# Linear attention with key sums from a constant channel, key-value products through the weights, and no token-major v

## The chip, the cores and the metric

The kernel is written for one Trainium2 chip and runs on one of its cores. The metric is the device time of one execution in microseconds. An execution has one launch and ends when the last output block has been written to HBM. The profile is of one such execution; its engines are TensorE (PE, with its weight loads apart as PEld), VectorE (DVE), ScalarE (ACT), GpSimd (POOL) and SyncE (SP), which here only issues transfers.

## The reference

The input is 32 sequences of 256 tokens with 128 channels, all float32. One transformer layer is computed:

```
h   = layernorm(x)                       # over the 128 channels, no gain, no offset
q,k,v = h Wq^T, h Wk^T, h Wv^T           # 8 heads of 16
q,k = rope(q), rope(k)
kv  = sum_s k_s v_s^T ; ksum = sum_s k_s ; vsum = sum_s v_s     # per sequence and head
a_s = (q_s kv / 4 + vsum) / (q_s . ksum / 4 + 256)
o   = (a + depthwise_conv5(v) + lepe_b) * (h Wg^T)
x2  = x + o Wo^T
out = x2 + (fp8 product of layernorm(x2) with the 128x128 ffn weights, to bf16) + ffn_b
```

Two identities are at work in the change. Layernorm output sums to zero over its channels, so W h does not change if the same column is subtracted from every column of W; with column 0 subtracted, channel 0 no longer counts and may hold anything. And with vm = vsum / 256, a_s = vm + (q_s (kv - ksum vm^T) / 4) / (q_s . ksum / 4 + 256).

## The kernel before, in words

A unit u is two sequences, that is four tiles of 128 tokens; there are 16 units (U). Every stage is a small helper of one engine that takes u, waits on semaphores for its inputs and for its buffers to come free, works on all of the unit and signals. The order in which an engine calls its helpers is written out by hand in each of the five engine blocks (`@block.tensor`, L1079 on, and so on): a beginning with its own order, a loop in the middle (`for t in range(6, 12)` on TensorE, L1320, with `project_g(t - 3)` as its first call), and the last units written out again. So TensorE works at the same time on units t, t - 1, t - 2, t - 3 and t - 4, and each queue runs strictly in its order.

The stages of one unit, with the engine and the line of the helper's work:

- SyncE loads x (`load_x`, L240) into one of four slots and stores the result (`store`).
- `stats1` (VectorE, L803) takes mean and variance, `var_eps1` (ScalarE, L293/L294) prepares them, `pow1` (GpSimd, L543/L546) computes 1/sqrt and the offset, `norm1` (ScalarE, L303) writes h, token-major.
- `transpose_h` (TensorE, L1112) turns it; `move_hT` (ScalarE, L315) copies it to SBUF channel-major as hT, two halves of 256 tokens, and sums each over the tokens as it goes (hsum).
- `project_qk` (TensorE, L1122), once for each sequence j: hT tiles as weights, 256 columns of joint q and k weights moving, token-major result. `rope` (VectorE, L812) multiplies by cosines and sines, `add_rope` (GpSimd, L583) adds the pairs.
- `project_v` (TensorE, L1133): four products with hT tiles as weights, giving v token-major; `move_v` (ScalarE, L323) copies it to SBUF; `transpose_v` (TensorE, L1149) turns it into v channel-major in PSUM, on which the five-tap convolution works: `conv_outer` and `conv_middle` (ScalarE, L333, L342), three `conv_tap` (VectorE, L827) and `sum_outer` (GpSimd, L595). `conv_middle` adds lepe_b as its bias.
- `transpose_q` (L1157) and `move_qT` (ScalarE, L349) give q channel-major.
- `key_value` (TensorE, L1168): k tiles as weights against v with eight columns of ones beside it, accumulated over two tiles of a sequence, so kv and ksum in one; `mask_kv` (VectorE, L838) keeps the blocks of each head.
- `sum_v` (TensorE, L1179) writes vsum to all tokens of the numerator: hsum broadcast as weights, twice 272 columns moving, `start=True`; `attend` (L1187) adds q kv on it with `start=False`. `invert` (VectorE, L844/L847) takes 1/den, `divide` (L854) gives t1.
- `transpose_t1` (TensorE, L1196), `add_lepe` (VectorE, L862), `project_g` (TensorE, L1141, one 512-column product), `gate` (VectorE, L871), `project_o` (TensorE, L1206), `residual` (VectorE, L879).
- The second half: `stats2` (L889), `var_eps2`, `pow2` (L554), `norm2` (L367), `transpose_h2` (L1215), `quantise_if_small` (L398), `ffn` (L1249), `move_y` (L405), `add_bias` (L602), `final_sum` (L609).

A product of float32 tiles shows as two matmul instructions with a weight load each, a transpose as one. PSUM has eight banks. The numerator p_num has two of its own; the other six are shared by turns between the rest, and the extra waits that TensorE's calls carry, as in

```
project_v(t - 1, (hT_done, count_first(t - 1)))
transpose_v(t - 1, (tap_done[-1], count(t - 2)))
sum_v(t - 2, (t1_done, count_last(t - 3)))
attend(t - 2)
```

name who must have read a bank before it is written again. VectorE's loop is `stats1(t)`, `add_lepe(t-3)`, `gate(t-3)`, `rope(t-1,1)`, `mask_kv(t-2)`, `residual(t-3)`, `stats2(t-3)`, `conv_tap(t-1,0)`, `rope(t-1,0)`, `invert(t-2)`, `conv_tap(t-1,1)`, `divide(t-2)`, `conv_tap(t-1,2)`. ScalarE's is `norm2`, `move_v`, `quantise_if_small`, `var_eps1`, `conv_middle`, `move_y`, `conv_outer`, `norm1`, `move_qT`, `var_eps2`, `move_hT`. At the start SyncE issues its transfers in the order x of unit 0 in two halves, ident, turn (the cosines and sines, 512 KB), wo, x of unit 1, conv_w, conv_b, mask, four small loads for the ffn, x of unit 2, x of unit 3; ScalarE's queue issues wq, wk, wv, wg. TensorE first keeps itself busy with 13 products of zeros, then turns the weights (L1088 to L1095).

## Time and profile before

| | |
|---|---|
| time, median of 3 runs | 175.99 us (175.90 to 176.16) |
| time of the profiled execution | 175.88 us |
| its span, first to last instruction | 174.1 us |
| TensorE busy | 161.3 us (93%), 1140 instructions |
| VectorE busy | 151.9 us (87%), 281 |
| GpSimd busy | 137.1 us (79%), 163 |
| ScalarE busy | 132.5 us (76%), 358 |
| chain that ended last | TensorE 83%, VectorE 6% |
| mean granted clock of TensorE | 0.976 |

Times are microseconds from the start of the span. A matmul's duration in the trace includes the time until its result is in PSUM, so neighbours overlap; what one costs in a full stream is the difference between starts. The same holds, by about 0.1 us, for ScalarE. "Idle before <- releaser" is the wait ahead of a group of instructions and who ended it.

### The profile page before, as it was taken

What the parts mean: (1) busy time and instruction counts of PE and PEld (TensorE: products, weight loads), DVE (VectorE), ACT (ScalarE), POOL (GpSimd) and SP (SyncE); (2) the same over time, 40 slices, a digit from 0 to 9 for tenths busy, and PEclk for the clock granted to TensorE, in tenths of its full rate; (3) what the DMA queues carried; (4) which work ended last, traced back from release to release, by engine and by line L of the source; (5) the groups of instructions that cost most, each with busy time, mean ns of one, the idle gap of its engine ahead of it and who ended that gap; (6) DMA issues with size and microseconds to landing.
All of it is one profiled execution on the core that took longest, in us unless ns stands there. A gap on an engine that the chain in (4) does not pass through costs nothing.

```text
span 174.1 us, 3891 instructions
## 1 busy us (share of the span) xinstructions
PE 161.3 (93%) x1140; PEld 137.5 (79%) x1140; DVE 151.9 (87%) x281; ACT 132.5 (76%) x358; POOL 137.1 (79%) x163
## 2 busy tenths in 40 slices
PE   7796999999999999999999999999999999998740
PEld 2475799797989898998989898989987897977510
DVE  2279999989998999999999999899898999999734
ACT  3668495787988878896969888676867797796671
POOL 1438698888989888989898888996979568987871
PEclk9999999999999999999999999999999999999955
DMA  4840002004040404021030404030040210100224
GB/s 121 241 122 0 0 6 60 2 0 124 2 120 6 120 0 120 6 76 48 21 101 0 124 2 120 6 101 20 2 124 0 85 43 0 49 15 2 60 60 121
DMA packets 18966, 9.71 MB, mean 56 GB/s; under 512 B 1536, under 2 KB 18816, under 8 KB 18944
## 3 DMA queue, kind: packets, MB, share of 16 engines
q1 hardware_dynamic: 18368, 9.19, 18.3%
q10 hardware_dynamic: 576, 0.26, 0.6%
q8 instruction: 10, 0.16, 0.4%
q14 instruction: 12, 0.10, 0.2%
HBM read 5.25 MB, written 4.19 MB: 54 GB/s over the span
## 4 chain that ended last, share of the span: by engine, by line
PE 83%; DVE 6%; SPq 3%; issue 2%; DMA 2%; POOL 1%; ACT 1%; DVEq 0%; ACTq 0%; POOLq 0%
PE bank L1122 14%; PE p_num L1187 9%; PE bank L1168 8%; PE bank L1206 8%; PE p_num L1179 8%; PE bank L1133 8%; PE bank L1141 8%; PE bank L1157 4%; PE bank L1196 4%; PE bank L1149 4%; PE bank L1112 4%; DMA xs<-_attn_hidden_states_dram 2%; PE bank L1249 2%; PE bank L1215 2%; DVE turned L812 1%
## 5 line engine op out<-in xcount | busy, mean ns | idle before, releaser
L583 POOL TENSOR_TENSOR qk<-turned 128x512 f32<-128x512 f32 x32 | 40.3, 1275 | 2.4 <-DVE turned L812 2.2
L812 DVE TENSOR_TENSOR turned<-bank,turn 128x1024 f32<-128x1024 f32 x32 | 38.6, 1215 | 0.7 <-PE bank L1122 0.3
L827 DVE SCALAR_TENSOR_TENSOR acc<-bank,conv_w,acc 128x510 f32<-128x510 f32 (+1 forms) x48 | 34.7, 722 | 0.5 <-ACT acc L342 0.4
L1122 PE MATMUL bank<-w_qk,hT 128*128 128x256 f32 x128 | 32.7, 380 | 0.0
L367 ACT ACTIVATE h<-x,nmr,rs 128x128 bf16<-128x128 f32 x60 | 24.7, 482 | 6.4 <-POOL nmr L557 6.3
L303 ACT ACTIVATE h<-xs,nmr,rs 128x128 f32<-128x128 f32 x64 | 26.3, 486 | 0.7 <-POOL nmr L546 0.7
L543 POOL TENSOR_TENSOR rs<-ve,minus_half 128x4 f32<-128x4 f32 (+1 forms) x17 | 16.6, 975 | 10.7 <-ACT ve L294 10.5
L595 POOL TENSOR_TENSOR acc<-acc,outer 128x508 f32<-128x508 f32 x16 | 20.3, 1268 | 5.8 <-DVE acc L827 5.7
L1122 PEld LDWEIGHTS bank<-w_qk,hT 128*128 128x128 f32 x128 | 22.4, 191 | 2.4 <-issue 0.2
L554 POOL TENSOR_TENSOR rs<-ve,minus_half 128x4 f32<-128x4 f32 (+1 forms) x17 | 16.6, 977 | 8.5 <-ACT ve L358 8.5
L1133 PEld LDWEIGHTS bank<-w_v,hT 128*128 128x128 f32 x128 | 16.5, 192 | 5.0 <-issue 4.3
L1187 PE MATMUL p_num<-kvs,qT 128*128 128x136 f32 x128 | 18.2, 284 | 0.4 <-DVE kvs L838 0.4
L602 POOL TENSOR_TENSOR yc<-yb,fb 128x512 bf16<-128x512 bf16 x15 | 17.3, 1153 | 1.2 <-ACT yb L405 1.2
L609 POOL TENSOR_TENSOR ob<-x,yc 128x512 f32<-128x512 f32 x15 | 17.4, 1159 | 0.9
L1206 PE MATMUL bank<-w_o,oT 128*128 128x128 f32 x128 | 17.3, 277 | 0.8 <-DVE oT L871 0.8
L1168 PE MATMUL bank<-v,qk 128*128 128x136 f32 x128 | 17.7, 281 | 0.1
L1179 PE MATMUL p_num<-w_v,hsum 128*128 128x272 f32 x64 | 17.4, 394 | 0.0
L398 ACT ACTIVATE q<-bank,rsc 128x512 fp8e4<-128x512 bf16 x15 | 10.3, 685 | 9.3 <-PE bank L1215 9.3
L1133 PE MATMUL bank<-w_v,hT 128*128 128x128 f32 x128 | 16.9, 275 | 0.0
L1187 PEld LDWEIGHTS p_num<-kvs,qT 128*128 128x128 f32 x128 | 16.1, 190 | 0.9 <-issue 0.8
L1206 PEld LDWEIGHTS bank<-w_o,oT 128*128 128x128 f32 x128 | 15.7, 192 | 1.3 <-DVE oT L871 1.3
L1141 PE MATMUL bank<-hT,w_g 128*128 128x512 f32 (+1 forms) x34 | 16.4, 570 | 0.0
(88 smaller groups left out, 326.6 us busy)
## 6 DMA issues: line engine op xcount, KB each, us to landing
xs<-_attn_hidden_states_dram SPq DMA_DIRECT2D x15, 256.0 KB, 2.8
out_dram<-ob SPq DMA_DIRECT2D x15, 256.0 KB, 2.5
turn<-in_turn_dram SPq DMA_DIRECT2D x1, 512.0 KB, 5.3
xs<-_attn_hidden_states_dram SPq DMA_DIRECT2D x2, 128.0 KB, 2.7
out_dram<-ob SPq DMA_DIRECT2D x2, 128.0 KB, 2.1
mask<-in_mask_dram SPq DMA_DIRECT2D x1, 68.0 KB, 4.3
w_raw<-in_L_attn_Wq_dram ACTq DMA_DIRECT2D x1, 64.0 KB, 2.3
w_raw<-in_L_attn_Wk_dram ACTq DMA_DIRECT2D x1, 64.0 KB, 2.4
```

The costliest lines, as they stand in the source:

```text
L303: last = nc.scalar.activation(h[:, s, t], xs[:, u % NX, t], ACT.Identity, scale=rs1[:, s, t:t + 1], bias=nmr1[:, s, t:t + 1])
L367: last = nc.scalar.activation(h2[:, s, t], x2[:, u % 3, t], ACT.Identity, scale=rs2[:, s, t:t + 1], bias=nmr2[:, s, t:t + 1])
L583: nc.gpsimd.tensor_tensor(qk[:, u % 2, j].rearrange("p q t d -> p t q d"), turned[:, j, :, :, 0:D].rearrange("p a h (q d) -> p (a h) q d", ...
L812: nc.vector.tensor_tensor(turned[:, j], p_qk[j].rearrange("p a h d -> p a (h d)").unsqueeze(2).to_broadcast([P, TPB, 2, 2 * D]), turn[:], ...
L827: nc.vector.scalar_tensor_tensor(out=part, in0=p_vT[:, :, lo + off:hi + off], scalar=conv_w[:, k:k + 1], in1=part, op0=ALU.mult, op1=ALU.a ...
L1122: last = nc.tensor.matmul(p_qk[j][:, a].rearrange("p h d -> p (h d)"), hT[:, u % 3, t * P:(t + 1) * P], w_qk[:].rearrange("p a q d -> p (a ...
L1133: last = nc.tensor.matmul(p_v[:, t], hT[:, u % 3, t * P:(t + 1) * P], w_v[:, 0:D], start=True, stop=True)
L1141: nc.tensor.matmul(p_gT[:] if j is None else p_end_gT[j], w_g[:], hT[:, u % 3, part_of(j)], start=True, stop=True).then_inc(gT_filled, 1)
L1168: last = nc.tensor.matmul(p_kv[:, t // TPB], qk_tile(u, 1, t), v[:, u % 3, t], start=(t % TPB == 0), stop=(t % TPB == TPB - 1))
L1179: nc.tensor.matmul(p_num[:, TPB * j:TPB * (j + 1), 0:NW], hsum[:, u % 3, j:j + 1].to_broadcast([P, P]), w_v[:].unsqueeze(1).to_broadcast([ ...
L1187: last = nc.tensor.matmul(p_num[:, t, 0:NW], qT[:, u % 2, t * P:(t + 1) * P], kvs[:, u % 2, t // TPB], start=False, stop=(t % TPB == TPB - 1))
L1206: last = nc.tensor.matmul(dst[:, n], oT[:, u % 2, t * P:(t + 1) * P], w_o[:], start=True, stop=True)
```

## The change

- `norm1` writes channels 1 to 127 of h only; channel 0 of all slots is set to one at the start, and h has three slots. The weights Wq, Wk, Wv and Wg have their column 0 subtracted on VectorE before they are turned (`subtract_first`, four instructions).
- `project_v` is one product with w_v as weights and 512 columns of hT moving, whose result is v channel-major in PSUM. `move_v`, `transpose_v` and the tile v are gone.
- `sum_v` computes the sum of v twice: as rows (33 output partitions, 128 columns) and as columns (128 partitions, 2 columns). `move_row` (ScalarE) writes the rows, times -1/256, into row 0 of w_kv, a copy of w_v per slot and sequence with eight more columns that are 1 in row 0 and 0 elsewhere. `move_col` writes lepe_b plus the columns over 256 into `bias`, which `conv_middle` adds, now as one instruction per sequence.
- `gather` (TensorE) takes h token-major as weights against k: kh, 128 channels by 128, per sequence, in which row 0 is the sum of k; `move_kh` (ScalarE) copies it; `key_value` is one product kh x w_kv per sequence, which gives kv - ksum vm^T and the sum of k in the eight columns.
- `attend` has no base written before it (`start=True`).
- PSUM is one tensor of eight banks with new sharing: kh is in bank 0 and q turned in bank 1, the two banks of p_num; `project_qk(.,0)` has bank 4, `project_qk(.,1)` bank 2 with t1 turned and the ffn result; the sums bank 5; kv, hT and h2 turned bank 7; the gate and `project_o` bank 6; v bank 3.
- All engines have new orders, SyncE's first loads too.

The diff, cut to its core:

```diff
@@ SyncE, first loads
             sp.dma_start(ident[:], ident_c).then_inc(wqk_in, 16)
+            for dst, src in ((conv_w[:], lepe_w.rearrange("c a k -> c (a k)")),
+                             (conv_b[:], lepe_b.rearrange("(c a) -> c a", a=1))):
+                sp.dma_start(dst, src).then_inc(c_in, 16)
             sp.dma_start(turn[:], turn_c).then_inc(turn_in, 16)
-            sp.dma_start(w_raw[:, 4], wo).then_inc(w_in, 16)
             load_x(1)
...
+            load_x(2)
+            sp.dma_start(mask[:], mask_c).then_inc(c_in, 16)
+            sp.dma_start(w_raw[:, 4], wo).then_inc(wo_in, 16)
@@ ScalarE
-                    last = nc.scalar.activation(h[:, s, t], xs[:, u % NX, t], ACT.Identity, scale=rs1[:, s, t:t + 1],
-                                                bias=nmr1[:, s, t:t + 1])
+                    last = nc.scalar.activation(h[:, u % 3, t, 1:D], xs[:, u % NX, t, 1:D], ACT.Identity,
+                                                scale=rs1[:, s, t:t + 1], bias=nmr1[:, s, t:t + 1])
...
-            def move_v(u):
...
+            def move_row(u):
+                act.wait_ge(vsum_filled, count(u))
...
+                for b in range(BPU):
+                    last = nc.scalar.activation(w_kv[0:1, u % 2, b, 0:D], p_vsum[ROW * b:ROW * b + 1, 0:D], ACT.Copy,
+                                                scale=-1.0 / S)
+                last.then_inc(row_done, 1)
+
+            def move_col(u):
...
+                nc.scalar.activation(bias[:, u % 2], p_vsum[:, D:D + BPU], ACT.Identity, scale=1.0 / S,
+                                     bias=conv_b[:, 0:1]).then_inc(col_done, 1)
+
+            def move_kh(u):
+                act.wait_ge(kh_filled, count(u))
+                if u >= 2:
+                    act.wait_ge(kv_filled, count(u, 2))
+                nc.scalar.activation(kh[:, u % 2], p_kh, ACT.Copy).then_inc(kh_done, 1)
...
-                nc.scalar.activation(acc[:, u % 2], p_vT, ACT.Identity, scale=conv_w[:, TAPS // 2:TAPS // 2 + 1],
-                                     bias=conv_b[:, 0:1]).then_inc(tap2_done, 1)
+                act.wait_ge(col_done, count(u))
+                for b in range(BPU):
+                    last = nc.scalar.activation(acc[:, u % 2, b], p_vT[:, b], ACT.Identity,
+                                                scale=conv_w[:, TAPS // 2:TAPS // 2 + 1],
+                                                bias=bias[:, u % 2, b:b + 1])
+                last.then_inc(tap2_done, 1)
@@ ScalarE, loop
-            for t in range(5, 12):
+            for t in range(6, 12):
                 norm2(t - 4)
-                move_v(t - 1)
+                move_col(t - 1)
                 quantise_if_small(t - 4, is_small)
                 var_eps1(t)
+                conv_outer(t - 1)
                 conv_middle(t - 1)
                 move_y(t - 4)
-                conv_outer(t - 1)
+                move_kh(t - 2)
+                move_qT(t - 2)
                 norm1(t)
-                move_qT(t - 2)
                 var_eps2(t - 3)
+                move_row(t - 1)
                 move_hT(t)
@@ GpSimd
+            def set_up_w_kv():
+                pool.wait_ge(v_ready, 1)
+                nc.gpsimd.tensor_copy(w_kv[:, :, :, 0:D].rearrange("p a b d -> p (a b) d"),
+                                      w_v[:].unsqueeze(1).to_broadcast([P, 2 * BPU, D])).then_inc(w_kv_done, 1)
...
+            for t in range(5, 12):
+                pow1(t)
+                add_bias(t - 4)
+                final_sum(t - 4)
+                pow2(t - 3)
+                add_rope(t - 1, 1)
+                add_rope(t - 1, 0)
+                sum_outer(t - 1)
@@ VectorE
+            def subtract_first(n):
+                nc.vector.tensor_scalar(w_diff[:, n], w_raw[:, n], w_raw[:, n, 0:1], None,
+                                        ALU.subtract).then_inc((diff_qk_done, diff_vg_done)[n // 2], 1)
...
             stats1(0, 0)
             stats1(0, 1)
+            difference_qk()
+            difference_vg()
             set_up_qk()
             set_up_v()
             set_up_g()
             stats1(1)
+            rope(0, 0)
+            stats1(2)
+            rope(0, 1)
             set_up_o()
-            stats1(2)
-            rope(0, 0)
-            rope(0, 1)
...
+            for t in range(6, 13):
                 stats1(t)
                 add_lepe(t - 3)
                 gate(t - 3)
-                rope(t - 1, 1)
-                mask_kv(t - 2)
+                rope(t - 1, 0)
+                conv_tap(t - 1, 0)
                 quantise_if_wide(t - 4, is_small)
                 residual(t - 3)
+                mask_kv(t - 2)
                 stats2(t - 3)
-                conv_tap(t - 1, 0)
-                rope(t - 1, 0)
+                rope(t - 1, 1)
                 invert(t - 2)
                 conv_tap(t - 1, 1)
                 divide(t - 2)
                 conv_tap(t - 1, 2)
@@ TensorE
-                for t in range(TPU):
-                    last = nc.tensor.matmul(p_v[:, t], hT[:, u % 3, t * P:(t + 1) * P], w_v[:, 0:D], start=True, stop=True)
-                last.then_inc(v_filled, 1)
+                nc.tensor.matmul(p_vT.rearrange("p j s -> p (j s)"), w_v[:], hT[:, u % 3], start=True,
+                                 stop=True).then_inc(vT_filled, 1)
...
+                nc.tensor.matmul(p_vsum[0:ROW + 1, 0:D], hsum[:, u % 3], w_v[:], start=True, stop=True)
+                nc.tensor.matmul(p_vsum[:, D:D + BPU], w_v[:], hsum[:, u % 3, ::ROW], start=True,
+                                 stop=True).then_inc(vsum_filled, 1)
...
+            def gather(u, *freed):
...
+                for t in range(TPU):
+                    last = nc.tensor.matmul(p_kh[:, t // TPB], h[:, u % 3, t], qk_tile(u, 1, t),
+                                            start=(t % TPB == 0), stop=(t % TPB == TPB - 1))
+                last.then_inc(kh_filled, 1)
...
+                for b in range(BPU):
+                    last = nc.tensor.matmul(p_kv[:, b], kh[:, u % 2, b], w_kv[:, u % 2, b], start=True, stop=True)
+                last.then_inc(kv_filled, 1)
@@ TensorE, loop
             for t in range(6, 12):
                 project_g(t - 3, (x2_done, count_last(t - 4)))
-                project_v(t - 1, (hT_done, count_first(t - 1)))
-                project_qk(t - 1, 1, (rope_done[1], count(t - 2)))
-                transpose_t1(t - 3, (qT_done, count(t - 3)))
-                transpose_h2(t - 4, (v_done, count(t - 1)))
-                transpose_v(t - 1, (tap_done[-1], count(t - 2)))
-                key_value(t - 2, (rope_done[0], count(t - 2)))
-                ffn(t - 4, is_small, (q8_done, count(t - 4)))
-                transpose_q(t - 2, (t2_done, count_last(t - 3)))
+                project_qk(t - 1, 0, (rope_done[0], count(t - 2)))
+                sum_v(t - 1, (row_done, count(t - 2)), (col_done, count(t - 2)))
+                transpose_t1(t - 3, (rope_done[1], count(t - 2)))
+                transpose_h2(t - 4, (hT_done, count_first(t - 1)))
+                project_v(t - 1, (tap_done[-1], count(t - 2)))
+                transpose_q(t - 2, (t1_done, count_last(t - 3)))
+                ffn(t - 4, is_small, (t2_done, count_last(t - 3)))
+                gather(t - 2, (t1_done, count_last(t - 3)))
                 project_o(t - 3, (oT_done, count_last(t - 3)))
-                sum_v(t - 2, (t1_done, count_last(t - 3)))
-                project_qk(t - 1, 0, (kvs_done, count(t - 2)))
-                transpose_h(t, (yb_done, count(t - 4)))
-                attend(t - 2)
+                key_value(t - 2, (q8_done, count(t - 4)))
+                project_qk(t - 1, 1, (yb_done, count(t - 4)))
+                attend(t - 2, (kh_done, count(t - 2)), (qT_done, count(t - 2)))
+                transpose_h(t, (kvs_done, count(t - 2)))
@@ TensorE, last unit
-            project_g(15, (tap_done[-1], count(15)), j=0)
-            project_g(15, (rope_done[1], count(15)), j=1)
-            transpose_t1(15, (qT_done, count(15)), j=0)
+            project_g(15, (rope_done[0], count(15)), j=0)
+            key_value(15, (q8_done, count(12)))
             project_o(14, (oT_done, count_last(14)))
-            attend(15, 0)
-            transpose_h2(13, (yb_done, count(12)))
-            attend(15, 1)
-            ffn(13, is_small, (q8_done, count(13)))
+            attend(15, (kh_done, count(15)), j=0)
+            transpose_h2(13, (kvs_done, count(15)))
+            attend(15, (qT_done, count(15)), j=1)
+            transpose_t1(15, (t1_done, count_last(15, j=0)), j=0)
+            ffn(13, is_small, (t2_done, count_last(14)))
             transpose_t1(15, (x2_done, count_last(14)), j=1)
+            project_g(15, (q8_done, count(13)), j=1)
+            project_o(15, (yb_done, count(13)), j=0)
```

## Rows read from the trace of the kernel before

**Rows 1.** By stretch: us; TensorE, its loads, VectorE, ScalarE, GpSimd busy; clock, DMA share, GB/s.

```profile
0.00:11.65 11.65, 9.50 (x41) 5.71 (x42) 3.65 (x12) 5.75 (x17) 3.50 (x16) 1.00 0.67 181
11.65:31.00 19.35, 17.41 (x118) 14.65 (x118) 18.56 (x34) 14.35 (x42) 14.71 (x20) 1.00 0.05 15
31.00:106.70 75.70, 75.48 (x560) 67.16 (x559) 72.13 (x128) 64.59 (x176) 66.57 (x71) 1.00 0.19 55
106.70:161.04 54.34, 53.51 (x392) 46.70 (x392) 50.72 (x95) 41.35 (x108) 44.73 (x48) 1.00 0.13 39
161.04:174.10 13.06, 5.35 (x32) 3.29 (x32) 6.83 (x17) 6.42 (x16) 7.58 (x11) 0.68 0.28 80
```

**Rows 2.** TensorE in order of time, one unit: start, duration, line, tile, count.

```profile
87.67 1.02 PE L1141 MATMUL bank<-hT,w_g 128*128 128x512 f32 x2
88.53 1.05 PE L1133 MATMUL bank<-w_v,hT 128*128 128x128 f32 x8
89.42 1.03 PE L1122 MATMUL bank<-w_qk,hT 128*128 128x256 f32 x4
90.29 0.60 PE L1196 MATMUL bank<-ident,t 128*128 128x128 f32 x4
...
90.95 0.61 PE L1149 MATMUL bank<-ident,v 128*128 128x128 f32 x4
91.39 1.09 PE L1168 MATMUL bank<-v,qk 128*128 128x136 f32 x8
92.32 0.39 PE L1249 MATMUL bank<-fwq,q 128*128 128x128 bf16 x4
...
93.02 1.06 PE L1206 MATMUL bank<-w_o,oT 128*128 128x128 f32 x8
93.92 1.08 PE L1179 MATMUL p_num<-w_v,hsum 128*128 128x272 f32 x4
94.83 1.03 PE L1122 MATMUL bank<-w_qk,hT 128*128 128x256 f32 x4
95.70 0.60 PE L1112 MATMUL bank<-ident,h 128*128 128x128 f32 x4
96.13 1.13 PE L1187 MATMUL p_num<-kvs,qT 128*128 128x136 f32 x8
97.10 1.02 PE L1141 MATMUL bank<-hT,w_g 128*128 128x512 f32 x2
```

**Rows 3.** ScalarE in order of time, the same unit.

```profile
89.83 0.57 ACT L323 ACTIVATE v<-bank 128x512 f32<-128x512 f32 x1
...
92.08 0.77 ACT L342 ACTIVATE acc<-bank,conv_b,conv_w 128x512 f32<-128x512 f32 x1
...
93.33 0.68 ACT L333 ACTIVATE outer<-bank,conv_w 128x508 f32<-128x508 f32 x1
...
96.33 0.38 ACT L315 ACTIVATE hT<-bank 128x256 f32<-128x256 f32 x1
...
96.97 0.20 ACT L315 ACTIVATION_READ_ACCUMULATOR hT<-bank 128x1 f32 x1
```

**Rows 4.** VectorE in order of time, the same unit; in brackets the idle time before.

```profile
93.39 0.43 DVE L838 TENSOR_TENSOR kvs<-bank,mask 128x272 f32<-128x272 f32 x1
94.12 0.69 DVE L879 TENSOR_TENSOR x<-bank,xs 128x512 f32<-128x512 f32 x1 [0.29 <-PE bank L1206]
```

**Rows 5.** VectorE in order of time, the start; in brackets the wait and its releaser.

```profile
10.97 0.76 DVE L803 BATCH_NORM_STATS2 st<-xs 128x6 f32<-128x256 f32 x2 [1.26 <-DMA xs<-_attn_hidden_states_dram]
11.65 2.34 DVE L812 TENSOR_TENSOR turned<-bank,turn 128x1024 f32<-128x1024 f32 x2
```

**Rows 6.** SyncE's queue in order of time: the issues of x of units 2 and 3.

```profile
7.07 0.98 SPq L240 DMA_DIRECT2D xs<-_attn_hidden_states_dram  x2
```

**Rows 7.** DMA issues: queue, count, KB, us from issue to landing.

```profile
w_raw<-in_L_attn_Wg_dram ACTq DMA_DIRECT2D x1, 64.0 KB, 4.8
```

**Rows 8.** VectorE in order of time, the end.

```profile
162.40 0.42 DVE L862 TENSOR_TENSOR t<-bank,acc 128x256 f32<-128x256 f32 x1 [0.79 <-PE bank L1196]
```

715 lines of the change are left out of this document (366 added, 349 removed).

## The prediction

> **What bounds the kernel now.** I read the stretches first, then TensorE's order of time, then the other engines beside it. From 31 to 106.7 us TensorE is busy 75.48 of 75.70 us, VectorE 72.13, GpSimd 66.57 and ScalarE 64.59 [rows 1]. That stretch is eight units (a unit is two sequences, 512 tokens), so TensorE is the bound, and VectorE is only 0.4 us a unit behind it. One unit of the repeated schedule takes 97.10 - 87.67 = 9.43 us between two starts of the gate projection [rows 2], with no hole in it. On VectorE the same unit shows one wait, 0.29 us for `project_o` [rows 4]; so VectorE alone would need 9.43 - 0.29 = 9.14 us for a unit, and that is the first floor under whatever TensorE saves. Two other places matter: the start, where VectorE's first `rope` begins at 11.65 us, and the end, 13.06 us in which TensorE is mostly idle [rows 1].
>
> **TensorE's work, part by part.** Times are differences of starts in [rows 2], since the engine is pipelined. `project_v` goes from 8 instructions of 128 columns (89.42 - 88.53 = 0.89) to one 512-column product, for which `project_g` is the row: 88.53 - 87.67 = 0.86. `transpose_v` goes: 91.39 - 90.95 = 0.44. `key_value` falls from four tiles to two products of the same shape, 0.93 to 0.47, but `gather` is new: four accumulating 128-column tiles, as the old `project_v`, 0.90. `sum_v` falls from four passes of 272 columns (94.83 - 93.92 = 0.91) to one 128-column pair (0.22) and one pair of two columns. No row has two columns; it costs nothing if it hides wholly, and at most what a 128-column pair costs, 0.22, plus 0.10 if the load behind it shows. I take 0.24, near the top, because the weights it loads are full tiles. Sum before 0.89 + 0.44 + 0.93 + 0.91 = 3.17, after 0.86 + 0.47 + 0.90 + 0.46 = 2.69: 0.48 us less a unit, 8.95 in place of 9.43, and 7.7 us over sixteen units. All other products keep their shapes.
>
> In the trace weight loads cost almost nothing beside a product: `project_g` streams its 512 columns with 2 loads in 0.86, the old `project_v` the same columns with 8 loads in 0.89 [rows 2]. The Trainium skill, TensorE: Matmul & The Clock Gate, section Measured speedup vs the span model, says a load overlaps a running matmul only where the two use different row groups. By that rule the six loads a unit that go (24 to 18) would give back their own time too, about 0.1 us each, and the unit would fall by some 0.6 us more; these rows, all of full tiles, speak against it, and the sum would be the same by both, since TensorE is no longer the bound after the change.
>
> **ScalarE.** `move_v` (0.57 [rows 3], some 0.50 of it its own after overlap) goes. `move_kh` copies half as much: the half-width copy of `move_hT` takes 0.38, some 0.28 of it its own. `move_row` is two instructions of 128 elements on one partition, `move_col` one of two elements; the bounds are the one-element 0.20 and the 256-element 0.38 [rows 3], and with the overlap of neighbours I take 0.2 each, 0.6 together, near the short row. `conv_middle` in two halves: 0.77 as one, so two of about 0.55 that overlap by 0.1, 0.25 more. Net 0.28 + 0.60 + 0.25 - 0.50 = 0.63 more a unit. ScalarE was busy 64.59 / 8 = 8.07 us a unit [rows 1], so 8.7: still under the others, but no longer loose.
>
> The Trainium skill, ScalarE: Activation LUTs, section What ACT_TABLE_LOAD costs, states 186 ns plus 0.833 ns per element, 93 ns more for each per-partition pointer, and 93 ns of overlap. By it one `move_row` instruction would occupy 200 ns, and a half of `conv_middle` 490 ns, which puts the split at 0.31 us more rather than 0.25; the row of the whole (0.77) stands a little under the page's figure for it (0.80). By the page the sum would be 0.06 x 12 = 0.7 us longer, if ScalarE lies on the ring.
>
> **VectorE and GpSimd.** Their work a unit is unchanged; GpSimd's is 66.57 / 8 = 8.3 us. Once, at the start, VectorE subtracts column 0 from four weight matrices, each 128 columns, so under the 0.43 of `mask_kv` with 272 [rows 4] and over nothing; I take 0.25, 1 us together, most of it in time in which it waits for data (3.65 busy of 11.65 [rows 1]). GpSimd's copy of w_v into four slots (512 columns) I put at 1.2 us, over the 66.57 / 71 = 0.94 of its mean instruction, which takes the tiny ones in [rows 1]; it lies in an idle stretch (3.50 busy of 11.65) but is queued ahead of `pow1(1)`, so unit 1's normalisation waits for it, and its transposes for that.
>
> **Does the saving reach the end?** TensorE's 8.95 is under VectorE's 9.14, so VectorE or a ring of waits sets the unit. I follow two rings through the new loop. The first starts when `mask_kv` has ended: `attend` 0.97, `transpose_h` 0.43, `move_hT` (96.13 to 97.17 [rows 2, 3]) 1.04, `project_qk` half 0 0.87, `sum_v` 0.46, `transpose_t1` and `transpose_h2` 90.95 - 90.29 = 0.66, `project_v` 0.86, `ffn` and `transpose_q` 93.02 - 92.32 = 0.70, `gather` 0.90, `project_o` 0.90, 0.20 until `residual` starts, then 0.69 for it and 0.43 for `mask_kv` [rows 4]: 9.1 us. In it TensorE waits 0.2 us for `move_hT`, because only `project_g` (0.86) stands between the transposes and their use, where before `attend` stood there too. The second leaves through ScalarE: after `project_v` 0.2, `conv_outer` 0.68 less 0.10 of overlap, then `conv_middle` and `move_y` 93.33 - 92.08 = 1.25 with 0.25 more for the split, `move_kh` 0.38 and 0.05 to be seen, `key_value` 0.47, `project_qk` half 1 0.87, then `attend` to `project_v` as above, 0.97 + 0.43 + 1.04 + 0.87 + 0.46 + 0.66 + 0.86: 9.3 us. So three things stand between 9.1 and 9.3; I take 9.25, 0.18 below now.
>
> **The sum.** Eight units at 0.18: 1.4. From 106.70 to 161.04, four to five units in a hand-written order, VectorE idles 54.34 - 50.72 = 3.6 us while TensorE has 53.51 of work [rows 1]; TensorE's share falls by 4 x 0.48 = 1.9, and I take two thirds, 1.3. From 11.65 to 31, VectorE idles 0.8: 0.2 of it. Start: `rope(0,0)` stands behind `stats1(2)`, which waits until 10.97 for a load issued only at 7.07 [rows 5, 6]. The change issues it six slots earlier and puts the first `rope` ahead of it. On SP's queue `turn` is then two slots later, about 1 us (0.98 for two issues [rows 6]), `load_x(1)` one and `wo` five, with its transpose taken out of the first chain; `mask` keeps its slot. What then ends last is the gate matrix, whose differences VectorE takes before it copies w_qk out: it is the fourth issue of ScalarE's queue, so issued near 2.1, and lands 4.8 later [rows 7], near 7; then `set_up_qk` near 7.8, first product 7.9, `rope` about 9.1, against 11.65. VectorE must also do `stats1(2)` (0.7) later, so the stream is 1.8 us ahead; bounds are 0 (the wait for the new gate-weight chain eats it) and 2.5 (all of it). End: `transpose_t1` is no longer behind both gate products, for which VectorE waited 0.79 [rows 8]: 0.5. Together 1.4 + 1.3 + 0.2 + 1.8 + 0.5 = 5.2 us. The profiled execution took 175.88 (span 174.10 and 1.78 around it), 0.11 under the median of 175.99; the sum from it is 170.7, from the median 170.8.
>
> **Rivals.** (a) VectorE's holes close fully. The units run at 9.14 (8 x 0.29 = 2.3), the late stretch gives 2.5, the start 2.3, the end 0.8: with 0.3 early, 8.2 us, about 167.8. For it: the orders of all engines are new. Against: both rings above are as long as VectorE's work, and each hand-over has to be met. (b) Only the start and the end gain. The unit stays at 9.43, since a ring takes TensorE's place exactly: 2.3 to 2.8 us, about 173.5. For it speaks how near 9.3 is to 9.43. (c) Slower: the ScalarE ring. One bank now holds first `kh`, then attention's numerator, and TensorE's in-order queue has `key_value` ahead of `project_qk`, `attend` and the next transposes, so each 0.1 us by which `move_kh` is late is 0.1 us a unit. Its reasons to be late are three small instructions and a split ahead of it. At a third of a microsecond more than my 9.3 the ring is 9.63; over twelve units that is 2.4 us lost, with no gain in the late stretch, against 1.0 gained at the start if that is short too: 177.4. It decides where twelve units' excess over 9.43 passes what start and end gain: from 9.51 a unit with 1.0 gained, from 9.62 with the 2.3 of my sum. Against it: these are instructions of 0.2 us, and ScalarE has over 0.5 us a unit idle. (d) The change doesn't do what it says for TensorE: the two-column product or a bank handed back late costs what was saved, TensorE stays the bound at 9.4, and the start is eaten by the longer weight chain: about 175.9.
>
> **How the numbers follow.** Forecast 0.60, at 170.8, its own range 169.2 to 172.6; (a) 0.15; (b) 0.12; (c) 0.10; (d) 0.03. The range takes in (b) and most of (a) and the low end of (c): 168.0 to 175.2. About 0.2% (0.35 us) is what a measurement of this kernel can tell from no change: faster 0.85 (forecast, (a), (b) less a little), same 0.04, slower 0.11.
>
> **What would show it.** Right: two starts of `project_g` in the middle of the loop 9.2 to 9.3 us apart; TensorE busy about 7 to 8 us less in all, with a hole of 0.2 us ahead of the first `project_qk` of a unit; VectorE busy over 97% there, its 0.29 us wait gone or under 0.1; `transpose_v` and `move_v` absent, `gather` at 0.90, `sum_v` near 0.46; the first `rope` near 9.1 us. Wrong: a period of 9.4 or more, with waits of TensorE on `kh` or of ScalarE on the sums; a first `rope` after 10.5; or a second product of `sum_v` that holds TensorE for 0.4 us.

## The result and the profile after

The changed kernel takes 178.38 us (median of 4 runs, 178.29 to 178.56) beside 175.94 for the kernel before (4 runs on the same chip): ratio 1.0137, interval 1.0121 to 1.0153. It is slower by 2.4 us, where 170.8 was forecast and 168.0 to 175.2 was the range. The profiled execution took 178.29, of which the span is 176.4.

From the page of the kernel after, its first line of busy times and its chain:

```profile
PE 162.9 (92%) x1044; PEld 122.2 (69%) x1044; DVE 152.4 (86%) x285; ACT 143.4 (81%) x422; POOL 138.5 (78%) x166
PE 72%; ACT 9%; issue 6%; DVE 6%; POOL 5%; ACTq 1%; DVEq 0%; POOLq 0%
```

TensorE has 96 instructions fewer and is busy 1.6 us longer than before (161.3). Its share of the last chain fell from 83% to 72%: 9% now leads through ScalarE and 6% is "issue". The middle stretch of [rows 1] on the kernel after (window and length; then busy time and count of PE, PEld, DVE, ACT, POOL; granted clock, DMA share, GB/s):

```profile
31.00:106.70 75.70, 73.91 (x490) 56.60 (x489) 69.35 (x122) 67.45 (x197) 63.44 (x68) 1.00 0.17 50
```

In the middle TensorE now idles 1.8 us, and yet VectorE does less in that stretch than before (69.35 against 72.13): fewer units pass. The granted clock is 1.00 there before and after, so it has no part in this.

The steady loop shows why. One unit of TensorE in order of time (start, duration, engine, line, operation, tile, shape, count):

```profile
88.40 0.60 PE L1189 MATMUL psum<-ident,h 128*128 128x128 f32 x4
88.84 1.02 PE L1226 MATMUL psum<-hT,w_g 128*128 128x512 f32 x2
89.93 1.13 PE L1199 MATMUL psum<-w_qk,hT 128*128 128x256 f32 x4
90.99 0.41 PE L1217 MATMUL psum<-w_v,hsum 128*33 128x128 f32 x2
91.33 0.38 PE L1218 MATMUL psum<-hsum,w_v 128*128 128x2 f32 x2
91.57 0.64 PE L1272 MATMUL psum<-ident,t 128*128 128x128 f32 x4
92.05 0.39 PE L1291 MATMUL psum<-identb,h 128*128 128x128 bf16 x4
92.27 1.08 PE L1209 MATMUL psum<-hT,w_v 128*128 128x512 f32 x2
93.19 0.60 PE L1234 MATMUL psum<-ident,qk 128*128 128x128 f32 x4
93.62 0.39 PE L1325 MATMUL psum<-fwq,q 128*128 128x128 bf16 x4
94.08 1.13 PE L1243 MATMUL psum<-qk,h 128*128 128x128 f32 x8
95.04 1.06 PE L1282 MATMUL psum<-w_o,oT 128*128 128x128 f32 x8
95.94 0.69 PE L1255 MATMUL psum<-w_kv,kh 128*128 128x136 f32 x4
96.46 1.03 PE L1199 MATMUL psum<-w_qk,hT 128*128 128x256 f32 x4
```

The next `project_g` starts at 98.71: 9.87 us a unit, against 9.43 before [rows 2] and 9.25 forecast. (These are single units from the middle of the loop; over the seven units from `divide(3)` to `divide(10)` the means are 9.83 and 9.51, so the loop as a whole lost 0.32 a unit.) By differences of starts: `project_g` 1.09, first `project_qk` 1.06, the two products of `sum_v` 0.58, `project_v` 0.92, `transpose_q` and ffn 0.89, `gather` 0.96, `key_value` 0.52. From [rows 2] I had priced them at 0.86, 0.87, 0.46, 0.86, 0.70, 0.90 and 0.47. The loads of the same unit say what stood there:

```profile
89.93 0.73 PEld L1199 LDWEIGHTS psum<-w_qk,hT 128*128 128x128 f32 x4 [0.90 <-ACT hT L335]
90.99 0.14 PEld L1217 LDWEIGHTS psum<-w_v,hsum 128*33 128x33 f32 x2 [0.33 <-issue]
94.05 0.97 PEld L1243 LDWEIGHTS psum<-qk,h 128*128 128x128 f32 x8 [0.21 <-issue]
```

The load for `project_qk` comes only when `move_hT` has signalled, 0.90 after the last load and when `project_g` (88.84 + 1.02) is over, so it lies beside no product; in the kernel before, `attend` stood in between and covered it. ScalarE in the same unit (start, duration, engine, line, tile):

```profile
89.04 0.38 ACT L335 ACTIVATE hT<-psum 128x256 f32<-128x256 f32 x1 [0.21 <-PE psum L1189]
...
89.41 0.38 ACT L335 ACTIVATE hT<-psum 128x256 f32<-128x256 f32 x1
...
93.40 0.67 ACT L371 ACTIVATE outer<-psum,conv_w 128x508 f32<-128x508 f32 x1
93.97 1.02 ACT L382 ACTIVATE acc<-psum,bias,conv_w 128x256 f32<-128x256 f32 x2
...
95.44 0.40 ACT L361 ACTIVATE kh<-psum 128x256 f32<-128x256 f32 x1
```

`move_kh` ends at 95.84 and `key_value` starts at 95.94, 0.90 after `project_o`, which is what `project_o` costs anyway: TensorE's own queue and the way through ScalarE arrive together. VectorE waits three times, where [rows 4] had one wait of 0.29:

```profile
92.25 0.69 DVE L960 TENSOR_TENSOR t<-psum,acc 128x512 f32<-128x512 f32 x1 [0.18 <-PE psum L1272]
95.02 0.75 DVE L925 SCALAR_TENSOR_TENSOR acc<-psum,conv_w,acc 128x510 f32<-128x510 f32 x1 [0.23 <-ACT acc L382]
96.14 0.69 DVE L977 TENSOR_TENSOR x<-psum,xs 128x512 f32<-128x512 f32 x1 [0.36 <-PE psum L1282]
```

The three waits are 0.77, and 9.87 less 0.77 is 9.10, so VectorE's list still is the 9.14 of the forecast. One hand-over from it is tight all the same: `residual` waits for `project_o` and starts at 96.14, `mask_kv` behind it ends at 97.17, and `attend`, which needs its result, loads its weights at 97.24.

Where the 2.3 us of span came from, by the starts of `divide` in both traces (there is one `divide` for each unit, numbered from 0, and the last is in two halves):

| stretch | before | after | difference |
|---|---|---|---|
| start to `divide(2)` | 42.17 | 40.08 | -2.1 |
| `divide(2)` to `divide(3)` | 8.99 | 10.61 | +1.6 |
| `divide(3)` to `divide(10)` | 66.58 | 68.82 | +2.2 |
| `divide(10)` to the last one | 43.45 | 44.70 | +1.3 |
| last `divide` to the end | 12.9 | 12.2 | -0.7 |

In unit 3 TensorE's order of time has two holes, around the hand-over from the beginning to the loop:

```profile
40.16 1.13 PE L1199 MATMUL psum<-w_qk,hT 128*128 128x256 f32 x4 [0.47 <-ACT hT L335]
47.29 1.09 PE L1263 MATMUL psum<-kvs,qT 128*128 128x136 f32 x8
48.69 0.65 PE L1189 MATMUL psum<-ident,h 128*128 128x128 f32 x4 [0.31 <-ACT h L322]
```

By the starts, `project_g` takes 1.49 there (38.67 to 40.16) where 0.86 is its row, and `transpose_h` starts 1.40 after `attend`, which takes 0.92 in the loop: about 1.1 us in the two.

### The profile page after: what moved, and what is told of

It is laid out like the page before. It is cut to its first block, busy times and chain, and to the rows that moved or that the text cites. A ratio compares the mean times of both kernels' runs of the same rounds, so it can differ in the third digit from the quotient of the medians.

```text
span 176.4 us, 3817 instructions
## 1 busy us (share of the span) xinstructions
PE 162.9 (92%) x1044; PEld 122.2 (69%) x1044; DVE 152.4 (86%) x285; ACT 143.4 (81%) x422; POOL 138.5 (78%) x166
## 4 chain that ended last, share of the span: by engine, by line
PE 72%; ACT 9%; issue 6%; DVE 6%; POOL 5%; ACTq 1%; DVEq 0%; POOLq 0%
PE psum L1199 15%; PE psum L1243 8%; PE psum L1209 8%; PE psum L1263 7%; PE psum L1282 7%; PE psum L1255 4%; PE psum L1189 4%; PE psum L1272 4%; PE psum L1234 3%; PE psum L1217 3%; ACT hT L335 3%; PE psum L1218 3%; PE psum L1226 3%; ACT h L322 2%; PE psum L1325 2%
## 5 line engine op out<-in xcount | busy, mean ns | idle before, releaser
L910 DVE TENSOR_TENSOR turned<-psum,turn 128x1024 f32<-128x1024 f32 x32 | 38.8, 1213 | 1.2 <-PE psum L1199 1.2
L925 DVE SCALAR_TENSOR_TENSOR acc<-psum,conv_w,acc 128x510 f32<-128x510 f32 (+1 forms) x48 | 34.7, 722 | 2.7 <-ACT acc L382 2.0
L1199 PE MATMUL psum<-w_qk,hT 128*128 128x256 f32 x128 | 34.2, 390 | 1.1 <-ACT hT L335 0.7
L1199 PEld LDWEIGHTS psum<-w_qk,hT 128*128 128x128 f32 x128 | 21.9, 190 | 10.4 <-ACT hT L335 8.3
L322 ACT ACTIVATE h<-xs,nmr,rs 128x127 f32<-128x127 f32 x64 | 26.5, 500 | 0.8 <-POOL nmr L624 0.8
L1243 PE MATMUL psum<-qk,h 128*128 128x128 f32 x128 | 17.6, 281 | 1.0 <-issue 0.7
L1263 PE MATMUL psum<-kvs,qT 128*128 128x136 f32 x128 | 18.0, 282 | 0.0
L1282 PE MATMUL psum<-w_o,oT 128*128 128x128 f32 x128 | 17.4, 277 | 0.1
L1209 PE MATMUL psum<-hT,w_v 128*128 128x512 f32 x32 | 16.9, 611 | 0.0
L1226 PE MATMUL psum<-hT,w_g 128*128 128x512 f32 (+1 forms) x34 | 16.7, 572 | 0.1
```

Of the source, the lines that this page charges most:

```text
L322: last = nc.scalar.activation(h[:, u % 3, t, 1:D], xs[:, u % NX, t, 1:D], ACT.Identity, scale=rs1[:, s, t:t + 1], bias=nmr1[:, s, t:t + 1])
L910: nc.vector.tensor_tensor(turned[:, j], p_qk[j].rearrange("p a h d -> p a (h d)").unsqueeze(2).to_broadcast([P, TPB, 2, 2 * D]), turn[:], ...
L925: nc.vector.scalar_tensor_tensor(out=part, in0=p_vT[:, :, lo + off:hi + off], scalar=conv_w[:, k:k + 1], in1=part, op0=ALU.mult, op1=ALU.a ...
L1199: last = nc.tensor.matmul(p_qk[j][:, a].rearrange("p h d -> p (h d)"), hT[:, u % 3, t * P:(t + 1) * P], w_qk[:].rearrange("p a q d -> p (a ...
L1209: nc.tensor.matmul(p_vT.rearrange("p j s -> p (j s)"), w_v[:], hT[:, u % 3], start=True, stop=True).then_inc(vT_filled, 1)
L1226: nc.tensor.matmul(p_gT[:] if j is None else p_end_gT[j], w_g[:], hT[:, u % 3, part_of(j)], start=True, stop=True).then_inc(gT_filled, 1)
```

## The experiments

All start from the changed kernel. Each median stands beside the kernel before on the same chip: 175.88 (7 runs) for the runs named a, 176.07 (15 runs) for b, 175.93 (13 runs) for c. The ratio is to that kernel; "less" and "more" are from the 178.38 of the changed kernel.

### One hole at a time

**a1_gather_first.** `gather` is put right behind `project_v`, to see whether the 0.22 that shows between ffn and `gather` goes and what that is worth.

```diff
-                transpose_q(t - 2, (t1_done, count_last(t - 3)))
-                ffn(t - 4, is_small, (t2_done, count_last(t - 3)))
                 gather(t - 2, (t1_done, count_last(t - 3)))
+                ffn(t - 4, is_small, (t2_done, count_last(t - 3)))
+                transpose_q(t - 2, (t1_done, count_last(t - 3)))
```

> Changed kernel with TensorE's loop (and the unit after it, seven units in all) calling gather, ffn, transpose_q in place of transpose_q, ffn, gather. Theory T (TensorE's own in-order stream is still the bound; every unit loses time in it where a load is not hidden): ffn to gather takes 0.46 us between starts where the kernel before has 0.24 from ffn to transpose_q, so a unit falls by 0.22, from 9.88 to 9.66, and the time by 1.5 us, to 176.9. Theory S (the ring through ScalarE, conv_outer to move_kh to key_value, sets the unit): move_kh starts only when move_y is done, so nothing moves, 178.4 within 0.4.

Measured 177.99, ratio 1.0121 (1.0104 to 1.0137). The edit did what it should to TensorE's order of time:

```profile
93.00 1.05 PE L1243 MATMUL psum<-qk,h 128*128 128x128 f32 x8
93.89 0.39 PE L1325 MATMUL psum<-fwq,q 128*128 128x128 bf16 x4
94.11 0.61 PE L1234 MATMUL psum<-ident,qk 128*128 128x128 f32 x4
94.56 1.06 PE L1282 MATMUL psum<-w_o,oT 128*128 128x128 f32 x8
95.71 0.73 PE L1255 MATMUL psum<-w_kv,kh 128*128 128x136 f32 x4
```

ffn now takes 0.22 and `gather` 0.89, and `project_o` begins 0.3 earlier; but `key_value` comes 1.15 behind it instead of 0.90. Its input `kh` is written no sooner. The unit is 9.84 to 9.85: the hole was moved, not closed, and 0.4 us in all came of it. So the ring through ScalarE is nearly as long as TensorE's queue.

**a2_cover_hT.** `transpose_h` ahead of `attend`, `norm1` ahead of `move_qT` on ScalarE: then `attend` hides `move_hT`, as in the kernel before.

```diff
-                attend(t - 2, (kh_done, count(t - 2)), (qT_done, count(t - 2)))
                 transpose_h(t, (kvs_done, count(t - 2)))
+                attend(t - 2, (kh_done, count(t - 2)), (qT_done, count(t - 2)))
...
-                move_qT(t - 2)
                 norm1(t)
+                move_qT(t - 2)
```

> Changed kernel with transpose_h ahead of attend on TensorE and norm1 ahead of move_qT on ScalarE, in the same seven units, so that attend and project_g both stand between the transposes and the first use of hT. Theory T: the wait for move_hT (0.23) and the unhidden load after it (first project_qk 1.06 against 0.87) go, 0.42 a unit, period 9.46, 2.9 us in all, 175.5. Theory S: the ring still passes attend, then project_g in place of the wait, and gains at most the 0.23, with norm1 now ahead of move_qT and attend waiting for it: 177 to 178.5.

Measured 178.10, 1.0125 (1.0108 to 1.0142). `project_g` is down to 0.86 and `project_qk` follows without a wait:

```profile
87.46 0.66 PE L1189 MATMUL psum<-ident,h 128*128 128x128 f32 x4
88.04 1.17 PE L1263 MATMUL psum<-kvs,qT 128*128 128x136 f32 x8
89.04 1.02 PE L1226 MATMUL psum<-hT,w_g 128*128 128x512 f32 x2
89.90 1.03 PE L1199 MATMUL psum<-w_qk,hT 128*128 128x256 f32 x4
90.86 0.41 PE L1217 MATMUL psum<-w_v,hsum 128*33 128x128 f32 x2
...
97.27 0.42 PEld L1189 LDWEIGHTS psum<-ident,h 128*128 128x128 f32 x4 [0.33 <-ACT h L322]
```

But TensorE now needs h earlier, and waits for it: the second `project_qk` takes 0.95 instead of 0.86 up to `transpose_h`, and that 0.58 instead of 0.44, with `move_qT` ending at 87.90 just ahead of `attend`. `attend` takes 1.00 instead of 0.92; that isn't a wait for ScalarE, since it takes 1.00 in a3 and c3 too, where q had long been copied, and its cause is open. The unit is 9.81. The edit opened other waits as it closed this one, and 0.06 us a unit was left of the gain.

**b1_both** takes both edits together.

> Changed kernel with the edits of a1 and a2 together. Theory R (several rings lie within 0.1 us of each other at 9.8: TensorE's stream; one through conv_outer, conv_middle, move_y, move_kh to key_value; one that goes on through norm1 and move_qT to attend): with gather early and hT covered, TensorE's stream would need 9.2, but the ring through norm1 and move_qT that a2 showed stays at 9.8, so the time stays near a2's, 177.6 to 178.1. Theory T alone (TensorE's stream bounds): the two savings add, 0.22 + 0.42 a unit, seven units, 173.9.

178.09 (2 runs), 9.81 a unit, 0.3 us less in all. That TensorE's own queue alone sets the unit is refuted: the hole behind ffn and the wait for `hT` are both closed, and `key_value` waits for `kh` (1.15 behind `project_o`) and `transpose_h` for h instead.

**b3_kh_before_y** adds to b1 the order `move_kh`, `move_y` on ScalarE, so that `key_value` gets its input first. Against the changed kernel ScalarE's part is:

```diff
-                move_y(t - 4)
                 move_kh(t - 2)
-                move_qT(t - 2)
+                move_y(t - 4)
                 norm1(t)
+                move_qT(t - 2)
```

> As b1, and in the same seven units ScalarE calls move_kh ahead of move_y. Theory R: kh is ready 0.6 us earlier, so key_value no longer waits, and the chain conv_outer, conv_middle, move_kh, move_y, norm1, move_qT is what is left ahead of attend; worked out from the rows of a1 and a2 the unit takes 9.5 us, 0.38 less than the changed kernel, 2.7 us in all, 175.7. Theory T alone: as b1, 173.9. If neither, and the chain through norm1 is as long as in a2: 177.6 to 178.1.

178.02, 1.0101 (1.0072 to 1.013): a miss, 2.3 above what was expected. `key_value` indeed waits no more (0.89 behind `project_o`), but now TensorE waits on another way through ScalarE, for `norm1`, and `transpose_h` starts 1.31 behind `project_qk` (95.81):

```profile
97.12 0.66 PE L1189 MATMUL psum<-ident,h 128*128 128x128 f32 x4 [0.29 <-ACT h L322]
```

The unit is 9.81 for the third time, after a2 and b1.

### The new small instructions

**a4_sum_twice** doubles both products of `sum_v`.

```diff
-                nc.tensor.matmul(p_vsum[0:ROW + 1, 0:D], hsum[:, u % 3], w_v[:], start=True, stop=True)
-                nc.tensor.matmul(p_vsum[:, D:D + BPU], w_v[:], hsum[:, u % 3, ::ROW], start=True,
-                                 stop=True).then_inc(vsum_filled, 1)
+                for _ in range(2):
+                    nc.tensor.matmul(p_vsum[0:ROW + 1, 0:D], hsum[:, u % 3], w_v[:], start=True, stop=True)
+                    last = nc.tensor.matmul(p_vsum[:, D:D + BPU], w_v[:], hsum[:, u % 3, ::ROW], start=True,
+                                            stop=True)
+                last.then_inc(vsum_filled, 1)
```

> Changed kernel with both products of sum_v issued twice. Theory T: TensorE pays all of it where it is the bound, 0.58 us a unit (the difference of starts from the first product of sum_v to transpose_t1), twelve to sixteen units, 7 to 9 us more, 185.4 to 187.7. Theory S: the ring that does not pass TensorE's sum_v first has slack, under 3 us more. If the price is less than 0.58 a unit with the unit's period growing by less, the excess over my 0.46 was the entry and exit of the pair, not its own time.

188.36, 1.0709 (1.0691 to 1.0727): 10.0 more, over the 7 to 9 expected, or 0.62 for each of the 16 units, the whole of what the second pair costs TensorE. The price of `sum_v` lies in full on the path; it is 0.58 to 0.62, not 0.46. Since every ring of waits in the loop passes `sum_v` on TensorE, this doesn't tell one ring from another.

**b2_columns_first** sets the two-column product, with its full tile as weights, ahead of the one with 33 columns as weights.

```diff
+                nc.tensor.matmul(p_vsum[:, D:D + BPU], w_v[:], hsum[:, u % 3, ::ROW], start=True, stop=True)
                 nc.tensor.matmul(p_vsum[0:ROW + 1, 0:D], hsum[:, u % 3], w_v[:], start=True,
-                                 stop=True)
-                nc.tensor.matmul(p_vsum[:, D:D + BPU], w_v[:], hsum[:, u % 3, ::ROW], start=True,
                                  stop=True).then_inc(vsum_filled, 1)
```

> Changed kernel with the two products of sum_v in the other order: first the two-column product (a full 128-column weight load), which then stands behind the 256-column project_qk, then the product with 33 weight columns. Theory L (a weight load is hidden only behind a long product; the two-column product hides nothing, and the load it needs is hidden only in part by 128 columns): sum_v falls from 0.58 to 0.40 to 0.46, and since doubling it cost its full 0.6 a unit in all sixteen units, the time falls by 1.9 to 2.9 us, to 175.5 to 176.5. Rival F (a fixed cost for each short instruction): the order does not matter, 178.4 within 0.3.

177.21, 1.0053 (1.0031 to 1.0075): 1.2 us less, under the 1.9 to 2.9 expected, and 9.76 a unit.

```profile
89.14 1.13 PE L1199 MATMUL psum<-w_qk,hT 128*128 128x256 f32 x4
90.11 0.28 PE L1217 MATMUL psum<-hsum,w_v 128*128 128x2 f32 x2
90.32 0.41 PE L1218 MATMUL psum<-w_v,hsum 128*33 128x128 f32 x2
90.65 0.66 PE L1272 MATMUL psum<-ident,t 128*128 128x128 f32 x4
```

`project_qk` takes 0.97 in place of 1.06 with the wait for `hT` still ahead of it, the pair 0.54 in place of 0.58. With a2, where it took 0.96 without a wait and with the old order behind it, this splits its excess: 0.09 to 0.10 belongs to the 33-column load behind it, and as much to the wait ahead. The two-column product (two instructions) costs 0.21 to 0.24.

**a3_one_middle** makes `conv_middle` one instruction again; both sequences then take the first one's bias, so the output for the second sequence of a unit has another mean of v.

```diff
-                for b in range(BPU):
-                    last = nc.scalar.activation(acc[:, u % 2, b], p_vT[:, b], ACT.Identity,
...
+                nc.scalar.activation(acc[:, u % 2], p_vT, ACT.Identity, scale=conv_w[:, TAPS // 2:TAPS // 2 + 1],
+                                     bias=bias[:, u % 2, 0:1]).then_inc(tap2_done, 1)
```

> Changed kernel with conv_middle as one instruction for both sequences (the second sequence gets the first one's mean of v as bias). 0.24 us a unit less on ScalarE, on the stretch from conv_outer to move_kh. Theory T: ScalarE is not on the ring, no change, 178.4 within 0.4. Theory S: 0.24 a unit over seven to twelve units, 1.7 to 2.9 us less, 175.5 to 176.7.

177.31, 1.0082 (1.0065 to 1.0099): 1.1 less, between the two expectations. The loop keeps 9.87 a unit (`project_g` at 88.24 and 98.11):

```profile
94.64 0.38 ACT L361 ACTIVATE kh<-psum 128x256 f32<-128x256 f32 x1
95.33 0.63 PE L1252 MATMUL psum<-w_kv,kh 128*128 128x136 f32 x4
```

`kh` is written at 95.02, 0.31 ahead of `key_value`, which stands 0.89 behind `project_o` and waits for nothing; so the way through ScalarE is cut by 0.3 and the unit stays as it was, held by TensorE's queue with the wait for `hT` in it. By the starts of `divide`, 0.5 of the 1.0 gained in the profile lies before the loop, 0.1 in it and 0.4 behind it.

### The start

**b4_old_start** gives SyncE's loads their old order and puts both `stats1` back ahead of the first `rope`.

```diff
-            for dst, src in ((conv_w[:], lepe_w.rearrange("c a k -> c (a k)")),
-                             (conv_b[:], lepe_b.rearrange("(c a) -> c a", a=1))):
-                sp.dma_start(dst, src).then_inc(c_in, 16)
             sp.dma_start(turn[:], turn_c).then_inc(turn_in, 16)
+            sp.dma_start(w_raw[:, 4], wo).then_inc(wo_in, 16)
             load_x(1)
-            load_x(2)
...
             stats1(1)
-            rope(0, 0)
             stats1(2)
+            rope(0, 0)
```

> Changed kernel with the start of the kernel before: SyncE loads in the old order (x of unit 2 in fourteenth place) and both stats1(1) and stats1(2) ahead of the first rope. divide(2) came 2.1 us earlier in the changed kernel than before; if that is the new start's doing and not the smaller work of the first units, this run is 1.5 to 2.1 us slower than the changed kernel, 179.9 to 180.5. If the first units' own work did it, under 0.5 us slower.

179.71 (2 runs), 1.3 above the kernel after; every `divide` from the first on is 1.5 later (22.19, 31.90, 41.59 against 20.68, 30.39, 40.08). So most of the 2.1 gained by `divide(2)` is these two edits together; they were not tried apart.

### Shortening what the rings share

In the changed kernel's own order TensorE's queue and the ways through ScalarE and VectorE all pass one station: from `transpose_h` through `move_hT` to `project_qk`. a2 took it off the path by an order that made TensorE wait for h; c1 leaves the order alone. `project_qk(.,0)` needs only the first half of hT, but waits for the signal of both.

**c1_half_hT** signals the first half by itself.

```diff
+                    if j is None and b == 0:
+                        last.then_inc(hT_half, 1)
                 last.then_inc(hT_done, 1)
...
-                pe.wait_ge(hT_done, count_first(u, j=j))
+                if j == 0 and u > 0:
+                    pe.wait_ge(hT_half, u)
+                else:
+                    pe.wait_ge(hT_done, count_first(u, j=j))
```

> Changed kernel in which move_hT also signals its first half, and project_qk of sequence 0 waits for that half only (sum_v and the other calls still wait for both). No work is taken away and no order is changed. Theory R (all the rings at 9.8 that pass project_g pass the wait for hT too, and the first load behind that wait is not hidden): the hole of 0.23 closes and project_qk falls from 1.06 towards 0.87, 0.3 to 0.4 a unit, and more where the wait was longer (8.3 us of waiting for hT stand in nine places of the profile), 3 to 4 us in all, 174.4 to 175.4. Rival V (VectorE's list, or the ring through norm1 and move_qT, is as long as these): under 1 us, 177.4 or more.

175.47, 0.9959 (0.9935 to 0.9983): 2.9 less than the kernel after, just short of the 3 to 4 expected, with no work taken away. From 77.60 to 106.14 three units take 9.51 each.

```profile
87.11 1.02 PE L1232 MATMUL psum<-hT,w_g 128*128 128x512 f32 x2
87.83 0.76 PEld L1205 LDWEIGHTS psum<-w_qk,hT 128*128 128x128 f32 x4 [0.53 <-ACT hT L336]
87.97 1.03 PE L1205 MATMUL psum<-w_qk,hT 128*128 128x256 f32 x4
```

The first load now lies beside `project_g`, and `project_g` takes 0.86.

**c2_half_columns** is c1 with the order of b2.

> c1 with the two-column product of sum_v first, as in b2. If the two savings lie on one ring they add: b2 gave 1.2 us, so 1.0 to 1.4 less than c1. If the time of c1 is set by another engine, under 0.4 less.

174.45, 0.9883 (0.9826 to 0.9941). The swap is worth 1.0 here, in the range expected, about what it gave alone.

**c3_all** adds to c2 the order of a1, `move_kh` ahead of `move_y` (but `attend` stays ahead of `transpose_h`, `move_qT` ahead of `norm1`), and `sum_v` behind `project_qk(.,0)` in units 11 and 13 of the late stretch:

```diff
-            sum_v(11, (row_done, count(10)), (col_done, count(10)))
             project_qk(11, 0, (rope_done[0], count(10)))
+            sum_v(11, (row_done, count(10)), (col_done, count(10)))
```

> c2 with gather ahead of ffn on TensorE and move_kh ahead of move_y on ScalarE in the seven units of a1, attend left ahead of transpose_h, and sum_v behind project_qk(.,0) in units 11 and 13. Theory R: the ring of project_v, conv_outer, conv_middle, move_kh, key_value, project_qk, attend, transpose_h, project_g, project_qk, sum_v, transposes sums to 9.1 from the rows of b3 and b2, which is VectorE's own list; a unit takes 9.15 to 9.25 in the loop, 1.5 to 2.5 less than c2, 171.5 to 172.7. If qT or the next h is late as in b3: no gain over c2.

172.61 (4 runs, 172.59 to 172.85), 0.9778 (0.9723 to 0.9833): 3.3 us faster than the kernel before and 5.8 faster than the one after. Its windows over the middle stretch and a unit of TensorE:

```profile
31.00:106.70 75.70, 75.05 (x515) 60.14 (x514) 72.85 (x130) 70.19 (x211) 66.44 (x73) 1.00 0.19 57
```

```profile
85.78 1.02 PE L1232 MATMUL psum<-hT,w_g 128*128 128x512 f32 x2
86.64 1.03 PE L1205 MATMUL psum<-w_qk,hT 128*128 128x256 f32 x4
87.50 0.28 PE L1223 MATMUL psum<-hsum,w_v 128*128 128x2 f32 x2
...
88.66 0.23 PEld L1297 LDWEIGHTS psum<-identb,h 128*128 128x128 bf16 x4 [0.19 <-ACT h L412]
...
95.04 1.02 PE L1232 MATMUL psum<-hT,w_g 128*128 128x512 f32 x2
```

9.26 us a unit, `project_g` and `project_qk` both at their full-stream 0.86, TensorE busy 75.05 of 75.70, VectorE 72.85. The order of a1, which gave 0.4 alone, and `move_kh` ahead of `move_y` give 1.8 together with the late edit, once the wait for `hT` is short. By the starts of `divide`, 1.2 of the 1.74 between the profiles of c2 and c3 lies in the six units from `divide(3)` to `divide(9)`, where only the orders changed, and 0.6 in the next one, where `sum_v(11)` stands too; behind it nothing changed (44.00 us from `divide(10)` to the last one in c2, 44.04 in c3), so the edit of unit 13 gave nothing. The two orders were not tried apart.

## Why the prediction was wrong

**TensorE's work, 0.48 less a unit: the step that failed.** The items were priced as differences of starts in a full stream [rows 2], and the new order doesn't have one: it has a wait ahead of `project_qk` and a product with 33 columns as weights behind it. The differences of starts of the profile after exceed my prices by 0.23 (`project_g`: the wait for `hT`), 0.19 (`project_qk`: half of it a load laid bare by that wait, half the 33-column load behind it), 0.12 (`sum_v`, taken at 0.46, near its upper bound, and 0.58), 0.19 (`transpose_q` and ffn, with what shows ahead of `gather`), 0.06 each (`gather`, `project_v`), 0.05 (`key_value`) and 0.04 (two transposes); `attend` took 0.05 less, 0.92 for 0.97. That is 0.89 altogether, against a saving of 0.48, and 8.95 + 0.89 = 9.84 is what this unit takes from `attend` to `attend`. With the holes closed a part of the saving exists: c3 takes 9.26, though not 8.95, so 0.17 a unit was there to be had and not 0.48. What c3 has over 8.95 is 0.18 in the two transposes (0.84 for 0.66, of which the wait for `norm2`'s h is the most), 0.09 in `sum_v` (0.55), 0.06 in `project_v` (0.92), 0.03 in `attend`, less 0.05 in the rest.

**The two rings.** The ring through ScalarE was found with its stations in the right order, and put at 9.34, rounded to 9.3. Measured on the same stations it is 9.84: `attend` to first `project_qk` 2.45 (2.44 in my working), `project_qk` 1.06 (0.87), `sum_v` 0.58 (0.46), the two transposes 0.70 (0.66), `project_v` to `attend` 5.05 (4.91, of which `project_v` to `conv_outer` is 1.13 for 1.06, ScalarE's four stages 2.44 for 2.46, the hand-over to `key_value` 0.10 for 0.05, `key_value` 0.52 for 0.47). ScalarE's own terms were right: its busy time in the middle is 67.45 over about 75.70 / 9.87 = 7.67 units, 8.79 a unit for 8.7. What was off by 0.5 is TensorE's share of the ring and the hand-overs. With the "0.2 us" wait for `move_hT` I saw the shared station and counted its wait, 0.2, but not that the load of the next product can't hide then. The first ring, put at 9.1, passes the same stations of TensorE: `attend` to `project_o` takes 7.56 for the 6.89 of the sum, `project_o` to the end of `mask_kv` 2.13 for 2.22, and 0.15 us later `attend` starts. So it too was 9.7 long, and three ways lay within 0.15 us of each other.

**Which rival came.** The outcome is that of (c), slower, with the unit past its deciding 9.51 to 9.62; but its reason, a late `move_kh` behind small instructions, is only one of the ways that tie. a1 shows that way holding the unit; a3 and b3 show that it isn't alone: with `kh` 0.3 early the unit keeps 9.87 in a3, and 9.81 in b3. (d), TensorE at 9.4 as the bound, is nearer in kind (the price of `sum_v` and bare loads ate what was saved) and too small in size. The chance for both, 0.13, rested on a margin of 0.13 us between the ring at 9.3 and the old unit (0.09 before rounding, since the terms add up to 9.34); the terms that I summed had more error than that in sum, since almost all erred to the same side.

**The weights' loads.** Six loads a unit fewer gave nothing back: 512 columns of `project_v` with 2 loads take 0.92 between starts here and took 0.89 with 8 [rows 2]. In the changed kernel itself `project_v` with 2 loads takes 0.92 and `gather`, as many columns with 8 loads, 0.89 where nothing stands ahead of it (a1). So the rule of the Trainium skill, TensorE: Matmul & The Clock Gate, section The mechanism (the prediction names the section behind it), that loads hide only behind other row groups doesn't show for a stream of full tiles; the same section also has loads into a background weight buffer pulled ahead, which would fit these rows, though no run here tests it. The loads that do show here are the one behind a wait and those of the product with 33 columns as weights.

**The split of `conv_middle`.** The two halves and `move_y` take 93.97 to 95.44, 1.47, against 1.25 as one [rows 3] and 1.27 in a3: 0.20 to 0.22 more, which agrees with my 0.25 from the rows. By the Trainium skill, ScalarE: Activation LUTs, What ACT_TABLE_LOAD costs, an estimate is one more fixed cost with two pointers less one overlap, 0.28; the 0.31 of the prediction set the page's halves against the row of the whole.

**Start and end.** The first `rope` starts at 9.44 (forecast 9.1, before 11.65), and `divide(2)` is 2.1 ahead, 1.8 forecast; b4 gives 1.3 to 1.5 of it to the two edits. The end gave 0.7 for 0.5. These two terms held, and were lost behind `divide(2)`: -2.8 at the ends, +5.1 between. The start came near its number by another path than forecast, which is luck in part: the four differences took 4.73 to 5.60 and w_qk was copied at 6.53 (7.8 forecast), so the gate matrix held nothing up. The transposes of unit 0 waited for h until 7.56, the first product started at 8.05, and `rope` then stood behind `stats1(1)` (8.76 to 9.52) in VectorE's order.

**What stays open.** Between ffn and `gather` 0.22 us shows as "issue" alone. Unit 3's two holes are named above and hold about 1.1 of its 1.6, but were not undone by themselves; c3 has 10.1 there (`divide(2)` at 40.05, `divide(3)` at 50.19), so they remain for the most part. The late stretch, 1.3 forecast as gain and 1.3 lost, was not taken apart; c1 brings it to 44.3 and c2 to 44.0, still over the 43.45 before. Which waits hold c3's unit between 9.26 and VectorE's 9.1 was not tested.
